# Expert rows turned by the DMA transfer as two planes of 16-bit halves, instead of on TensorE

## What is computed

```python
def expert_step(acc, inp):
    gu, dn, c = inp
    g = xf @ gu[:I].T
    u = xf @ gu[I:].T
    o = jax.nn.silu(g) * u @ dn.T
    return (acc + c[:, None] * o, None)
routed, _ = jax.lax.scan(expert_step, jnp.zeros_like(xf), (experts_gate_up, experts_down, combine.T))
```

## Time and profile before

| | us |
|---|---|
| median of 3 runs | 1335.8 (1335.38 to 1337.43) |
| profiled execution, its time | 1335.87 |
| its span | 1334.1 |
| attention, closing | about 140 to 860, 860 to 900 |
| 52 pairs | about 900 to 1057 |
| 88 whole tiles, 16 mixed | about 1057 to 1204, to 1244 |
| combine | 1247 to 1334 |

### The profile page before, as it was taken

The page is one execution under the profiler, slowest core; times in us unless marked ns, Lnnn a source line. Parts: engine busy times, 40 slices in busy tenths (PEclk is TensorE's granted clock), DMA queues, the critical chain, the costliest instruction groups (busy, mean ns, idle before and its releaser), DMA issues.

```text
span 1334.1 us, 26082 instructions
## 1 busy us (share of the span) xinstructions
PE 1283.5 (96%) x8098; PEld 637.6 (48%) x8098; DVE 1070.0 (80%) x2592; ACT 759.0 (57%) x1093; POOL 650.2 (49%) x964
## 2 busy tenths in 40 slices
PE   9996999999999999999999999999999999999895
PEld 6652322333323323323333232558888888885441
DVE  6878999999999999999999996475444566665497
ACT  4553777777676776777677768314444444446100
POOL 1004123335655755656466557756766655564100
PEclk8996999999999999999999999999999999999998
DMA  6777555534347256264363453768776665554798
GB/s 219 242 232 192 148 154 109 96 74 115 88 110 172 54 136 143 68 144 111 93 162 80 145 183 101 244 220 264 235 218 201 192 185 183 183 172 131 292 327 322
DMA packets 215235, 224.81 MB, mean 169 GB/s; under 512 B 109926, under 2 KB 177142, under 8 KB 214972
## 3 DMA queue, kind: packets, MB, share of 16 engines
q1 hardware_dynamic: 188524, 150.22, 41.9%
q0 software_dynamic: 21152, 66.10, 14.1%
q10 hardware_dynamic: 5424, 6.82, 1.5%
HBM read 127.33 MB, written 95.70 MB: 167 GB/s over the span
## 4 chain that ended last, share of the span: by engine, by line
PE 69%; DVE 10%; DMA 4%; POOL 4%; SPq 2%; issue 1%; ACT 1%; ACTq 0%; DVEq 0%; POOLq 0%
PE psO L1381 14%; PE psE L1368 13%; PE psM L1358 9%; PE ex_psGU L1969 7%; PE ex_psGU L2030 7%; DVE piece_max L1236 6%; PE ex_psY L2050 4%; PE ex_psY L1979 3%; DMA wide<-results 2%; PE psM L576 2%; PE ex_psX L2016 2%; PE ex_psX L1957 2%; SPq L144 2%; PE co_psS L2446 1%; PE psGU L1721 1%
## 5 line engine op out<-in xcount | busy, mean ns | idle before, releaser
L1236 DVE TENSOR_REDUCE piece_max<-psM 128x1 f32<-128x512 f32 x1008 | 631.0, 682 | 20.0 <-PE psM L1358 16.5
L1319 ACT ACTIVATE wide<-psE 128x1024 f32<-128x1024 f32 x512 | 497.1, 1021 | 186.9 <-PE psE L1368 184.6
L1368 PE MATMUL psE<-wide 49*128 49x512 bf16 (+1 forms) x2048 | 327.3, 379 | 5.0 <-DMA wide<-maxima 4.7
L1358 PE MATMUL psM<-wide 48*128 48x512 bf16 x1008 | 312.0, 389 | 11.7 <-DVE piece_max L1236 11.5
L1381 PE MATMUL psO<-wide 128*32 128x512 f32 x2048 | 273.2, 606 | 0.6 <-ACT wide L1319 0.6
L2261 POOL DMA_INDIRECT results<-vals_inv,places x208 | 200.3, 963 | 127.7 <-DVE vals_inv L2142 104.5
L1358 PEld LDWEIGHTS psM<-wide 48*128 48x128 bf16 x1008 | 76.4, 93 | 322.9 <-DVE piece_max L1236 271.4
L1368 PEld LDWEIGHTS psE<-wide 49*128 49x128 bf16 (+1 forms) x2048 | 118.0, 95 | 94.5 <-issue 11.9
L1455 POOL DMA_INDIRECT lists<-last_rows,slot x96 | 93.8, 977 | 52.6 <-issue 22.3
L1455 POOL DMA_INDIRECT lists<-rows,slot x96 | 94.6, 986 | 49.4 <-PE psO L1381 26.4
L2030 PE MATMUL ex_psGU<-wide,ex_xT 128*128 (+1 forms) x416 | 107.8, 382 | 0.8 <-ACT h2T L2103 0.8
(11 more groups left out here) (349 smaller groups left out, 1570.8 us busy)
## 6 DMA issues: line engine op xcount, KB each, us to landing
wide<-qk_parts SPq DMA_DIRECT2D x384, 64.0 KB, 2.7
wide<-results SPq DMA_DIRECT2D x16, 1536.0 KB, 9.8
qk_parts<-parts SPq DMA_DIRECT2D x32, 384.0 KB, 2.7
rows<-lists SPq DMA_DIRECT2D x26, 320.0 KB
h2Ts<-lists SPq DMA_DIRECT2D x26, 320.0 KB
xin<-in_x_dram SPq DMA_DIRECT2D x16, 512.0 KB, 4.0
wide<-in_guT_dram SPq DMA_DIRECT2D x3, 2560.0 KB, 9.9
rows<-lists SPq DMA_DIRECT2D x44, 160.0 KB
```

The costliest lines, as they stand in the source:

```text
L1236: v.tensor_reduce(piece_max[:, qh, (x * PAIRS + h) * KT // QH + qt, kh:kh + 1], bank_of("piece", PIECES * group + n), AX.X, ALU.max, negat ...
L1319: nc.scalar.activation(probs[:, step % 2, 2 * pair:2 * pair + 2], psE[:, pair], ACT.Exp, scale=HD ** -0.5).then_inc(exp_ok, 1)
L1358: nc.tensor.matmul(bank_of(*user), qa[g][rows, h, qt * P:(qt + 1) * P], ka[g][rows, h, kh * 512:(kh + 1) * 512], start=True, stop=True).th ...
L1368: mm = nc.tensor.matmul(psE[:, pair, x], k[g][part, pair, kt * P:(kt + 1) * P], q[g][part, pair, qh * 512:(qh + 1) * 512], start=(q is qa) ...
```

## The change

The layout of a list row in DRAM changes. The token's 256 float32 words are stored as two planes: first the 256 upper 16-bit halves, then the 256 lower ones. The 64 words of weights and destinations stay as they are.

- `planes(act, env, c)` is new: two ScalarE copies of 1024 16-bit elements for each partition. It runs once a chunk at `w` = 25 (and once in the closing phase for the last chunk), from `xhat` to `rows_of(c)`. The layer norm's last step now writes `xhat` in place, TensorE's `turn_half` reads `xhat`, and GpSimd's scatters and SyncE's `load_values` wait for `planes_ok` as well.
- For experts' rows SyncE issues two transfers instead of one. A transposing transfer of the 1024 bytes of both planes brings `[channel, plane and half of the channels, token]` into the buffer; an ordinary one brings the 256 bytes of weights and destinations. A mixed tile has four instead of two.
- ScalarE weaves the planes: two copies of 16-bit elements, each of which writes every second 16-bit place of `xT`, in place of one copy out of `psX`.
- TensorE's transposes into `psX` are gone, with `x_done`. VectorE and ScalarE wait for the rows' transfer itself, and SyncE frees a buffer by `x_ok`, which ScalarE raises after the second weaving copy.
- Before its first weaving copy ScalarE waits for the closing phase's last product.

```diff
@@ planes, new @@
+def planes(act, env, c):
+    act.wait_ge(env.h2_ok, c + 1)
+    if c > 1:
+        act.wait_ge(env.scattered[(c - 2) % CPB], 16 * TPC * TOPK * ((c - 2) // CPB + 1))
+    halves = env.xhat.bitcast(U16).rearrange("p i (d h) -> p i d h", h=2)
+    to = env.rows_of(c)[:, :, 0:D].bitcast(U16)
+    env.nc.scalar.activation(to[:, :, 0:D], halves[:, :, :, 1], ACT.Copy)
+    env.nc.scalar.activation(to[:, :, D:2 * D], halves[:, :, :, 0], ACT.Copy).then_inc(env.planes_ok, 1)
@@ SyncE, attention @@
-                    wait(sp, env.h2_ok, c)
+                    wait(sp, env.turned, KC * c)
+                    wait(sp, env.planes_ok, c)
@@ SyncE, experts @@
             def pair_of_tiles(t, u, row):
-                wait(sp, x_done, t - DEEP + 2)
+                wait(sp, x_ok, t - DEEP + 2)
                 wait(sp, dest_ok, t - DEEP + 2)
-                sp.dma_start(pair_rows[u // 2], env.lists[bass.ds(row, 2 * P)].rearrange("(j p) n -> p j n", p=P)
+                sp.dma_start_transpose(pair_planes[u // 2], in_planes[bass.ds(row, 2 * P), 0:2 * D]).then_inc(rows_in[u], 16)
+                sp.dma_start(pair_marks[u // 2], env.lists[bass.ds(row, 2 * P), D:ROW].rearrange("(j p) n -> p j n", p=P)
                              ).then_inc(rows_in[u], 16)
...
             def tile(t, u, row):
-                sp.wait_ge(x_done, t - DEEP + 1)
+                sp.wait_ge(x_ok, t - DEEP + 1)
                 sp.wait_ge(dest_ok, t - DEEP + 1)
-                sp.dma_start(rows[u], env.lists[bass.ds(row, P)]).then_inc(rows_in[u], 16)
+                sp.dma_start_transpose(tile_planes[u], in_planes[bass.ds(row, P), 0:2 * D]).then_inc(rows_in[u], 16)
+                sp.dma_start(marks[u], env.lists[bass.ds(row, P), D:ROW]).then_inc(rows_in[u], 16)
@@ TensorE, experts @@
             def pairs(p, v):
-                turn_pair(p, v)
                 if known(p - 1):
...
-                if exists(t):
-                    wait_rows(pe, t, u)
-                    wait(pe, x_ok, t - 1)
-                    for k in range(KC):
-                        mm = nc.tensor.transpose(psX[:, u % 2, k * P:(k + 1) * P], rows[u][:, k * P:(k + 1) * P],
-                                                 env.ident[:])
-                    mm.then_inc(x_done, 1)
@@ ScalarE, experts @@
             def copy_pair(p, v):
-                act.wait_ge(x_done, 2 * p + 2)
+                wait_pair_rows(act, p, v)
+                if p == 0:
+                    act.wait_ge(env.closing_y_done, env.closing_chunks)
                 wait(act, gu_done, 2 * p - 2)
-                nc.scalar.activation(xT[:, v % 2], psX[:, v % 2], ACT.Copy).then_inc(x_ok, 2)
+                to = xT[:, v % 2].bitcast(U16).rearrange("p (n t h) -> p n t h", n=KC, h=2)
+                nc.scalar.activation(to[:, :, :, 1], pair_planes[v][:, 0:KC], ACT.Copy)
+                nc.scalar.activation(to[:, :, :, 0], pair_planes[v][:, KC:2 * KC], ACT.Copy).then_inc(x_ok, 2)
...
                 if exists(t):
-                    act.wait_ge(x_done, t + 1)
+                    wait_rows(act, t, u)
                     wait(act, gu_done, t - 1)
-                    nc.scalar.activation(xT[:, u % 2, 0:D], psX[:, u % 2, 0:D], ACT.Copy).then_inc(x_ok, 1)
+                    to = xT[:, u % 2, 0:D].bitcast(U16).rearrange("p (n t h) -> p n t h", n=KC, h=2)
+                    nc.scalar.activation(to[:, :, :, 1], tile_planes[u][:, 0:KC], ACT.Copy)
+                    nc.scalar.activation(to[:, :, :, 0], tile_planes[u][:, KC:2 * KC], ACT.Copy).then_inc(x_ok, 1)
```

More of the change, by code:

```diff
@@ L11 @@
 I32 = mybir.dt.int32
+U16 = mybir.dt.uint16
 AX = mybir.AxisListType
@@ L1183, in scatter_step_by_step @@
             def scatter_step_by_step(c):
+                pool.wait_ge(env.planes_ok, c + 1)
                 for n in range(PORTIONS[0], PORTIONS[1]):
@@ L1307, in beside @@
                     half_scores(act, env, c, bank_of(c, w))
+                if c >= 0 and pair == 1 and w == SPLIT:
+                    planes(act, env, c)
             for n in range(HALF_PIECES):
@@ L1446, in pad @@
 def pad(eng, env, end):
-    eng.dma_start(env.lists[bass.ds(end, HALF)], env.pad_row[0:HALF]).then_inc(env.pads_out, 16)
+    eng.dma_start(env.lists[bass.ds(end, HALF)], env.pad_row[0:HALF].bitcast(I32)).then_inc(env.pads_out, 16)
 def scatter_chunk(nc, env, c, first=0, end=TPC * TOPK):
@@ L1536, in _ @@
             pool.wait_ge(env.routed, 1)
+            pool.wait_ge(env.planes_ok, LAST + 1)
             scatter_chunk(nc, env, LAST, 0, EARLY_LISTS)
@@ L1564, in _ @@
             half_scores(act, env, LAST, psGP[:])
+            planes(act, env, LAST)
             gate_shared(3, 1)
@@ L1799, in expert_phase @@
             "p (u n) -> p u n", n=ROW)
-        rows = [(env.rows if u < TPC else spare_rows)[:, u % TPC] for u in range(DEEP)]
-        pair_rows = [(env.rows if u < TPC else spare_rows)[:, u % TPC:u % TPC + 2] for u in range(0, DEEP, 2)]
+        both = [(env.rows if v < HALVES // 2 else spare_rows)[:, 2 * v % TPC:2 * v % TPC + 2].rearrange("p u n -> p (u n)")
+                for v in range(HALVES)]
+        pair_planes = [both[v][:, 0:2 * D].bitcast(U16).rearrange("p (n t) -> p n t", n=2 * KC) for v in range(HALVES)]
+        tile_planes = [both[u // 2][:, u % 2 * D:(u % 2 + 1) * D].bitcast(U16).rearrange("p (n t) -> p n t", n=2 * KC)
+                       for u in range(DEEP)]
+        pair_marks = [both[v][:, 2 * D:2 * ROW].rearrange("p (j n) -> p j n", j=2).bitcast(I32)
+                      for v in range(HALVES)]
+        marks = [pair_marks[u // 2][:, u % 2] for u in range(DEEP)]
+        in_planes = env.lists.bitcast(U16)
         xT = sb("ex_xT", [P, 2, KC * 2 * P])
@@ L1908, in tile, with half_tiles @@
             def tile(t, u, row):
-                sp.wait_ge(x_done, t - DEEP + 1)
+                sp.wait_ge(x_ok, t - DEEP + 1)
                 sp.wait_ge(dest_ok, t - DEEP + 1)
-                sp.dma_start(rows[u], env.lists[bass.ds(row, P)]).then_inc(rows_in[u], 16)
-            def half_tiles(t, u, *both):
-                sp.wait_ge(x_done, t - DEEP + 1)
+                sp.dma_start_transpose(tile_planes[u], in_planes[bass.ds(row, P), 0:2 * D]).then_inc(rows_in[u], 16)
+                sp.dma_start(marks[u], env.lists[bass.ds(row, P), D:ROW]).then_inc(rows_in[u], 16)
+            def half_tiles(t, u, *of_halves):
+                sp.wait_ge(x_ok, t - DEEP + 1)
                 sp.wait_ge(dest_ok, t - DEEP + 1)
-                for half, row in enumerate(both):
-                    sp.dma_start(rows[u][half * HALF:(half + 1) * HALF], env.lists[bass.ds(row, HALF)]
+                for half, row in enumerate(of_halves):
+                    sp.dma_start_transpose(tile_planes[u][:, :, half * HALF:(half + 1) * HALF],
+                                           in_planes[bass.ds(row, HALF), 0:2 * D]).then_inc(rows_in[u], 16)
+                    sp.dma_start(marks[u][half * HALF:(half + 1) * HALF], env.lists[bass.ds(row, HALF), D:ROW]
                                  ).then_inc(rows_in[u], 16)
@@ L2128, in dest @@
             def dest(u, h, *which):
-                both = rows[u][:, D:ROW].rearrange("p (k e) -> p k e", k=2)
+                both = marks[u].rearrange("p (k e) -> p k e", k=2)
                 for part, e in zip((slice(0, P),) if len(which) == 1 else (slice(0, HALF), slice(HALF, P)), which):
                     copy = nc.vector.tensor_copy(pair[part, DEEP * h + u].unsqueeze(2),
-                                                 both[part, :, bass.ds(e, 1)].bitcast(I32))
+                                                 both[part, :, bass.ds(e, 1)])
                 copy.then_inc(dest_ok, 1)
@@ L2506, in declare @@
     env.h2T_d = dram("turned", (LAST - 1, P, KC, CH), F32)
-    env.lists = dram("lists", (LIST_ROWS, ROW), F32)
+    env.lists = dram("lists", (LIST_ROWS, ROW), I32)
     env.table_d = dram("tile_table", (2 * P, 2), I32)
```

49 lines of the change are left out of this document (20 added, 29 removed).

## The result

| | before | after |
|---|---|---|
| median of 4 runs, us | 1336.62 (1335.38 to 1337.58) | 1438.97 (1435.37 to 1440.05) |
| span of the profiled execution | 1334.1 | 1438.3 |

The changed kernel is slower: ratio 1.078, 95% interval 1.076 to 1.080. The forecast was 1300 with a range up to 1410, so both the direction and the range were wrong.

What follows compares the result with a forecast made beforehand. TensorE was taken to bound the expert stages: 1335.9 - 45.3 (transposes) + 4.2 (attention) + 1 (GpSimd) + 4 (DMA unevenness) = 1299.8, so 1300 us. The range was 1288 to 1410, the forecast's own 1288 to 1312.

Steps and rivals of the forecast that it cites:

- the one on SyncE: Pair stage: SyncE waits 70.2 of 150 us, so two issues fit; a dearer transposing issue covered up to over 1 us.
- stays covered: Mixed tiles: ScalarE gains 0.38 us a tile on its 23.35 of 36 us, at no cost.
- Rival 1: Expert stages: transposing transfers become the DMA bound, pairs from T above 1.24; 1408 us at T = 2.5; chances 0.18, 0.15.
- the DMA term: Expert stages: DMA needs 2.36 of 2.60 us a pair, 1.10 of 1.41 a tile; 4 us added for unevenness.
- T: Time on all 16 DMA engines of a pair's transposing transfer, 256 x 1024 bytes; taken near 1.0 us, alternatives 1.82 and 4.5.
- some 800 us slower: Pair stage: case of eight 128x128 blocks transposed by DMA one after another at 1309 ns, 10.5 us a pair.
- TensorE's gain: Expert stages: transposes removed, 22.4 us in pairs and 22.9 in whole and mixed tiles, together 45.3 us.
- attention's cost: Attention: the two added plane copies delay exponentials by 0.6 us in each of seven chunks, 4.2 us.
- 2.20 forecast: ScalarE in a pair: two weaving copies at 0.60 each, plus 0.62 and 0.38, under TensorE's 2.60 us.
- rival 2: ScalarE in expert stages: weaving copies cost double, 1.20 us; decides from 0.80 a copy; around 1380 us, chance 0.07.
- the forecast's 1: Pair stage: GpSimd falls behind during the first 28 sends with their list scatters; cost 0 to 3, taken as 1 us.
- a slowdown through transfers: Slower through DMA up to 1410 (0.18), beyond that (0.15), or transfers cut in 32-byte pieces, about 2660 us (0.03).

Runs made afterwards that it cites:

- e5_marks_act: Changed kernel, but in 80 of the 88 whole tiles ScalarE instead of SyncE issues the marks' transfer; 1393.1 us, ratio to before 1.044.
- e2_half: Changed kernel with transposing transfers of the upper plane alone, half the bytes in as many instructions; 1433.7 us, ratio to before 1.073.
- e1_plain: Changed kernel with an ordinary transfer of the same bytes in place of each transposing one, marks still separate; 1317.1 us, ratio 0.986.
- e6_one_load: Changed kernel with one ordinary transfer of whole 1280-byte rows, marks included, in place of the transposing and the marks' transfers; 1294.6 us, ratio 0.971.
- e4_table: Changed kernel with SyncE's loads of row numbers from the tile table taken for two rounds at once; 1435.7 us, ratio to before 1.075.

## Why the prediction was wrong, step by step

**The step that failed is the one on SyncE:** "It waits 70.2 of 150 us ... so it has room for two issues a pair where one stood. A dearer issue for the transposing form is covered up to over 1 us." It failed three times.

- The price and the pace. An operation that no row showed was given one loose bound instead of two ends. It took 1.30 us where 0.38 stood, 0.92 more, and the marks' issue with its register work 0.6. The room was 70.2 / 49.5 = 1.4 us a pair against 1.5 needed. With the 0.43 us that TensorE gives up the room shrinks to 1.0: the paragraph counted it at the old pace. The excess of 0.5 on 2.60 gives 3.1 us; measured 160.1 / 52 = 3.08.
- The stage. The room was read in the pair stage alone. A tile has the same two issues for half the work. The same view of the kernel before, over 1062 to 1200, has

```profile
SPq L1910 <- DVE places L2131: 66.9, 62, 2.8
```

which is 66.9 / 84.7 = 0.8 us a tile, and 0.6 at the new pace, against 0.87 + 0.6 added. The excess of 0.9 on 1.41 gives 2.3 us; measured 210.8 / 88 = 2.40.
- The mixed tiles. Two issues became four: 2 x (1.17 + 0.47) and 0.8 between them is 4.1 us; measured 65.8 / 16 = 4.1. I wrote that a mixed tile "stays covered", looking at ScalarE only.

**Rival 1 had the right loss by the wrong mechanism, and the DMA term was too small as well.** It let the DMA engines run out. The transposing transfer's load on them can now be read. In e5_marks_act the marks go by ScalarE's queue, so that from 1080 to 1220 SyncE's queue carries the transposing transfers of 80 tiles alone:

```profile
q1 hardware_dynamic: 43027, 10.38, 37.3%
```

0.373 x 140 / 80 = 0.65 us of all 16 engines a tile, so T is about 1.3 us for the bytes of a pair. A second estimate is the difference between the changed kernel and e2_half from 1130 to 1250, the two rows above: (0.317 - 0.188) x 120 / 50 tiles = 0.31 us for half of a tile's bytes, so T is about 1.2. In the pair stage, where the DMA engines are fullest, the queue had

```profile
q1 hardware_dynamic: 67561, 18.40, 64.4%
```

from 908 to 1060, which is 0.644 x 3.08 = 1.98 us a pair; less my 0.60 for marks and pad rows, an estimated T of 1.4. There are 67561 packets for some 49.4 pairs, 1368 each. Without 256 for marks and some 36 for pad rows about 1080 remain, close to 1024 pieces of 256 bytes: the cutting that gave T = 1.82 in the prediction, at a lower price for each piece.

My T of 1.0 was therefore too low by 0.2 to 0.4, and it decides something. At 1.24 the prediction let the pair stage become bound by DMA. The stage's whole DMA work was forecast as 2.36 us a pair and measured as 0.94 x 3.08 = 2.9, more than the 2.60 of TensorE. e2_half shows that in this kernel the time does not follow the DMA work. With a cheaper issue the pair stage might still not have reached 2.60; no run shows that, since e1_plain and e6_one_load took the transposing transfer away with its issue.

The Trainium skill gives a transposing transfer 261 GB/s ("DMA: Bandwidth & Descriptors", "Latency and other measured facts"), by which T is an estimated 1.0; the traces here give 1.2 to 1.4. The Trainium skill's other figure, 1309 ns for a block ("VectorE: DVE Perf Modes", "The three transpose paths"), does not add up over a transfer's eight blocks: that would be 10.5 us, and the changed kernel's pairs come every 3.08. (The prediction's "some 800 us slower" for that case would be some 900 by rival 1's own formula, and its 1408 us at T = 2.5 is 1407.)

What I missed is what it costs the queue's engine to start such a transfer: for a tile 1.20 us against 0.6 of the 16 DMA engines' time, for a pair 1.30 against some 1.4.

**What held.** e6_one_load tests the rest of the sum without the transposing issue: forecast -45.3 + 4.2 + 1 for TensorE, attention and GpSimd, so 40.1 us less than before; measured 1294.6 us, 39.1 less than the 1333.7 us of the kernel before that was measured beside it. The closeness is partly luck: TensorE's gain was too large in the forecast by about 4 us and attention's cost by about 3.

- *TensorE.* Pairs -19.2 (22.4 forecast), whole tiles -16.1 (19.4), mixed -6.0 (3.5): 41.3 against 45.3.
- *Attention.* 4.2 us were forecast, 1.0 was paid. The last chunk's turned halves leave PSUM at 871.83 in the kernel before and at 872.84 in the changed one; the two rows:

```profile
871.83 1.09 ACT L620 ACTIVATE xin<-psT 128x512 f32<-128x512 f32 x2 [7.16 <-PE psT L586]
```

```profile
872.84 1.09 ACT L621 ACTIVATE xin<-psT 128x512 f32<-128x512 f32 x2 [6.98 <-PE psT L587]
```

The planes of the first chunk stand where they were expected, and the exponentials behind them run without a gap until they have caught up:

```profile
287.45 1.06 ACT L631 ACTIVATE rows<-vals_inv 128x1024 uint16<-128x1024 uint16 x1
288.40 1.06 ACT L632 ACTIVATE rows<-vals_inv 128x1024 uint16<-128x1024 uint16 x1
289.35 3.76 ACT L1336 ACTIVATE wide<-psE 128x1024 f32<-128x1024 f32 x4
```

- *ScalarE.* The weaving copies are dearer than the float32 ones, but not doubled; a pair's:

```profile
L2078 ACT ACTIVATE ex_xT<-rows x26: 767/778/783, 904.9 to 1055.3; 128x512 uint16<-128x512 uint16 x26
L2079 ACT ACTIVATE ex_xT<-rows x26: 740/746/758, 905.5 to 1055.9; 128x512 uint16<-128x512 uint16 x26
```

The durations of a pair sum to 0.78 + 0.75 + 0.60 + 0.37 = 2.50 us, against 2.20 forecast, but neighbours overlap. In e6_one_load, where TensorE sets the pace, the starts are:

```profile
960.76 0.77 ACT L2075 ACTIVATE ex_xT<-h2Ts 128x512 uint16<-128x512 uint16 x1
961.39 0.76 ACT L2076 ACTIVATE ex_xT<-h2Ts 128x512 uint16<-128x512 uint16 x1
962.01 0.61 ACT L2080 ACTIVATE h2T<-wide 128x512 f32 x1
963.07 0.38 ACT L2086 ACTIVATE act_s<-ex_psGU 128x256 f32<-128x256 f32 x1 [0.45 <-issue]
963.35 0.77 ACT L2075 ACTIVATE ex_xT<-h2Ts 128x512 uint16<-128x512 uint16 x1
```

The next pair begins after 963.35 - 960.76 = 2.59 us, with 0.45 of them idle. By starts a weaving copy costs some 0.63 us, far from rival 2's threshold of 0.80.
- *GpSimd* cost little: in e6's pair stage the excess over 52 x 2.60 = 135.2 is 3.5 us in all, start included, against the forecast's 1. It is already within the 19.2 us of the pairs.

**The chances.** 0.36 stood on a slowdown through transfers (0.18, 0.15 and 0.03), and only 0.18 beyond 1410. The range was built from one unknown, T. The second unknown of the same new instruction, its issue, had no share in it.

**What stays open.** Why the transposing issue takes 1.2 us whatever it moves is not shown, and neither is whether the DMA engines would hold the pair stage if it were cheap. Whether the transposing issue costs as much on ScalarE's queue was not tried, nor a kernel that uses the turned transfer for pairs alone: the tile stage would need the old layout of the rows.

## What to carry to other kernels

A DMA instruction has two prices, one for its queue's engine and one for the DMA engines; both need bounds when the form is new, and the first counts by instruction, in every stage that issues it, against the room that is left at the new pace. Waiting of a queue that is not on the chain is room only as long as the engine on the chain keeps its pace. Before taking work from the bound engine, list for each stage what every other sequencer spends for each tile, register loads included.

## What the runs showed of the hardware that was not expected

- A transposing transfer occupies SyncE, which issues it, for 1.17 to 1.31 us in the median, nearly independent of size (64 rows to 256 rows of 1024 bytes; 1.23 for 256 rows of 512 bytes). An ordinary one of rows or marks takes 0.33 to 0.48.
- The transposing transfers moved about 1080 packets for 256 KB, at an estimated 1.2 to 1.4 us of all 16 DMA engines.
- SyncE's load of numbers from SBUF into registers costs by the word: 16 took 3.7 us, 8 took 1.85, 4 took 1.04 (medians by stage, e4_table and the changed kernel).
- The granted clock of TensorE was lower where it idled. It was 1.00 throughout in the earlier trace rows, the 2.4 GHz level, and a mean of 0.96 over the whole tiles and 0.75 over the mixed ones after, where TensorE was 75% and 59% busy and the products on a mixed tile's second half had a median of 430 ns instead of 379. The mixed tiles' time is accounted for by SyncE's issues, so I see no cost of its own there.
